# Flamingo block with block-sparse feed-forward: tile 0's maxima added on TensorE instead of by DMA, tile 1's scores ahead of tile 2's queries, weights split one step later

## The reference

```python
q = layernorm(x); k = v = ctx                      # 16 heads of 16 features
s = q @ k.T / 4, masked causally                   # per head, 128 x 128
x = x + tanh(g_xattn) * softmax(s) @ v
n = layernorm(x)
mask = top_4_of_16(softmax(n @ w_router + b_router))      # blocks of 64 hidden units
x = x + tanh(g_ffn) * (relu(n @ w1.T + b1) * mask) @ w2.T + b2-term
```

## Time and profile before

| | before |
|---|---|
| median of 3 runs | 681.2 us (681.01, 681.2, 684.17) |
| profiled execution, own time | 680.97 us |
| span of its instructions | 679.1 us |
| granted TensorE clock, mean | 0.997 |
| TensorE matmul busy | 659.7 us, 97% |
| VectorE busy | 527.8 us, 78% |
| ScalarE busy | 538.9 us, 79% |
| GpSimd busy | 556.0 us, 82% |

### The profile page before, as it was taken

The page is one execution under the profiler, slowest core; times in us unless marked ns, Lnnn a source line. Parts: engine busy times, 40 slices in busy tenths (PEclk is TensorE's granted clock), DMA queues, the critical chain, the costliest instruction groups (busy, mean ns, idle before and its releaser), DMA issues.

```text
span 679.1 us, 30579 instructions
## 1 busy us (share of the span) xinstructions
PE 659.7 (97%) x12960; PEld 611.9 (90%) x12960; DVE 527.8 (78%) x1429; ACT 538.9 (79%) x785; POOL 556.0 (82%) x718
## 2 busy tenths in 40 slices
PE   6779999999999999999999999999999999999997
PEld 5668899999999999999999999989999999999997
DVE  6899887788777778788778878777878877877742
ACT  4668788888888888888888888888888888887732
POOL 6677888988988898888898898888888889887643
PEclk9899999999999999999999999999999999999999
DMA  5323355556545446645556654544554554553110
GB/s 197 96 55 86 88 109 99 116 109 115 120 114 116 99 110 116 111 112 113 100 117 107 116 111 122 103 107 114 113 113 112 116 100 96 98 86 64 28 40 32
DMA packets 192279, 69.24 MB, mean 102 GB/s; under 512 B 166160, under 2 KB 191888, under 8 KB 192144
## 3 DMA queue, kind: packets, MB, share of 16 engines
q1 hardware_dynamic: 191312, 65.72, 45.7%
q10 hardware_dynamic: 832, 1.57, 0.6%
HBM read 19.03 MB, written 8.39 MB: 40 GB/s over the span
## 4 chain that ended last, share of the span: by engine, by line
PE 86%; DVE 5%; DMA 3%; ACT 2%; issue 2%; POOL 1%; SPq 1%; POOLq 0%; DVEq 0%
PE bank L423 11%; PE score_banks L344 10%; PE bank L357 8%; PE score_banks L314 8%; PE bank L425 8%; PE bank L424 8%; PE bank L446 8%; PE bank L447 8%; PE bank L448 8%; PE bank L371 4%; PE bank L401 2%; PE score_banks L327 1%; DMA used_all<-used 1%; PE bank L393 1%; ACT weights L525 1%
## 5 line engine op out<-in xcount | busy, mean ns | idle before, releaser
L880 POOL TENSOR_TENSOR h_low<-hid,h_high 128x512 fp32r<-128x512 f32 x128 | 164.2, 1283 | 12.8 <-ACT hid L560 12.8
L738 DVE SCALAR_TENSOR_TENSOR hid<-bank,b_cols,used_all 128x256 f32<-128x256 f32 x248 | 108.1, 477 | 65.9 <-PE bank L425 58.2
L873 POOL TENSOR_SCALAR_AFFINE_SELECT weights<-weights 128x1024 f32<-128x1024 f32 x128 | 138.2, 1103 | 18.2 <-ACT weights L525 16.4
L423 PE MATMUL bank<-xT_high,w_high 128*128 128x256 f32 x496 | 151.5, 305 | 0.8 <-DVE hid L738 0.7
L525 ACT ACTIVATE weights<-score_banks 128x1024 f32<-128x1024 f32 x128 | 124.3, 1024 | 34.7 <-PE score_banks L344 34.6
L424 PE MATMUL bank<-xT_low,w_high 128*128 128x256 f32 x496 | 139.4, 281 | 0.0
L425 PE MATMUL bank<-xT_high,w_low 128*128 128x256 f32 x496 | 139.4, 281 | 0.0
L446 PE MATMUL bank<-w_high,h_high 128*128 128x256 f32 x488 | 137.3, 281 | 0.7 <-POOL h_low L880 0.7
L447 PE MATMUL bank<-w_low,h_high 128*128 128x256 f32 x488 | 137.7, 282 | 0.0
L448 PE MATMUL bank<-w_high,h_low 128*128 128x256 f32 x488 | 136.2, 279 | 0.0
L423 PEld LDWEIGHTS bank<-xT_high,w_high 128*128 128x128 f32 x496 | 93.3, 188 | 8.9 <-DVE hid L738 1.1
(11 more groups left out here) (105 smaller groups left out, 1411.1 us busy)
## 6 DMA issues: line engine op xcount, KB each, us to landing
x_in<-in_x SPq DMA_DIRECT2D x31, 256.0 KB, 3.1
out_y<-y_out SPq DMA_DIRECT2D x31, 256.0 KB, 2.2
c_in<-in_ctx SPq DMA_DIRECT2D x30, 256.0 KB, 2.8
qT<-qT SPq DMA_DIRECT2D x128, 4.0 KB
w_stage<-in_w1T ACTq DMA_DIRECT2D x1, 1024.0 KB, 9.2
hid<-in_w2T SPq DMA_DIRECT2D x8, 128.0 KB, 2.7
kT_parts<-k_parts SPq DMA_TRANSPOSE x57, 2.8
qT_parts<-q_parts SPq DMA_TRANSPOSE x57, 2.7
```

The lines of the kernel that those rows point to most:

```text
L423: pe.matmul(out=bank, lhsT=w1_high[:, k, c], rhs=high, start=k == 0, stop=False)
L738: dve.scalar_tensor_tensor(hid[:, n % 4, j], hid_bank(n)[:, j * TOKS:(j + 1) * TOKS], b1_cols[:, c:c + 1], used_all[:, p % 2], ALU.add, AL ...
L873: pool.affine_select(out=w, in_=w, compare_op=ALU.is_ge, fill=0.0, base=0, pattern=[[0, 2 * HB], [1, S]], channel_multiplier=-1).then_inc( ...
L880: pool.tensor_tensor(h_low[:, p % 2, chunks], hid[:, n % 4], h_high[:, p % 2, chunks].bitcast(F32), ALU.subtract).then_inc(h_low_made, 1)
```

## The change

For tile 0 alone the maxima no longer ride in tile 2's queries, and no DMA brings them. `row_maximum(0)` writes them into a tile of their own, `first_ride`, zero elsewhere. TensorE copies `qT` of tile 0 into a bank with one product by the identity (`first_again`) and accumulates onto it eight products of `first_ride` by halves of the identity (`first_maximum`). ScalarE copies the sum back over `qT` of tile 0 (`first_evacuated`). `shifted_scores(0)` waits for that copy, and so does the first `out_transposed`, which uses the same bank. In iteration 0 TensorE runs `scores(1)` ahead of the transposes of tile 2's queries. `max_row(0)` is gone from SyncE's queue. The pieces of the weights are taken in iterations 1 to 4, two each, and not in iterations 0 to 4.

```diff
+        first_ride = sb("first_ride", [P, HB, U, PAD], F32)
...
         def pieces_of(i):
-            return {0: (0, 1), 1: (2, 3), 2: (4, 5), 3: (6,), 4: (7,)}.get(i, ())
+            return {1: (0, 1), 2: (2, 3), 3: (4, 5), 4: (6, 7)}.get(i, ())
...
             def q_transposed(b):
                 pe.wait_ge(qn_made, b + 1)
-                if b >= MAX_LAG:
+                if b > MAX_LAG:
                     pe.wait_ge(max_found, b - MAX_LAG + 1)
...
+            def first_again():
+                pe.wait_ge(q_copied, 1)
+                pe.matmul(out=banks[M1][:], lhsT=ident[:], rhs=qT[:, 0, :], start=True, stop=False)
+
+            def first_maximum():
+                pe.wait_ge(max_found, 1)
+                for r in range(HB):
+                    f, t = divmod(r, 2)
+                    for g in range(2):
+                        turned = pe.matmul(out=banks[M1][:, r * S + g * HALF:r * S + (g + 1) * HALF],
+                                           lhsT=first_ride[:, 2 * t + g].rearrange("p u d -> p (u d)"),
+                                           rhs=ident[:, f * HALF:(f + 1) * HALF], start=False,
+                                           stop=r == HB - 1 and g == 1)
+                turned.then_inc(first_turned, 1)
...
             def shifted_scores(b):
                 s = b % TS
-                pe.wait_ge(max_landed[s], 2 * 16 * (b // TS + 1))
+                if b == 0:
+                    pe.wait_ge(first_copied, 1)
+                else:
+                    pe.wait_ge(max_landed[s], 2 * 16 * (b // TS + (1 if s else 0)))
...
                         q_transposed(i + 2)
+                    if i + 1 == 0:
+                        first_again()
                 else:
-                    if q_early(i + 2):
+                    if i > 0 and q_early(i + 2):
                         q_transposed(i + 2)
                     if i > 0 and k_early(i + 2):
                         k_transposed(i + 2)
                     if i + 1 < N:
                         scores(i + 1)
                     if i == 0:
+                        first_maximum()
+                        q_transposed(i + 2)
                         k_transposed(i + 2)
...
+            def first_evacuated():
+                act.wait_ge(first_turned, 1)
+                act.copy(qT[:, 0, :], banks[M1][:]).then_inc(first_copied, 1)
...
                 elif i >= 0:
+                    if i == 0:
+                        first_evacuated()
                     if q_early(i + 2):
...
-                ride = q_pad[:, carrier % QS, :, RIDE_COL].rearrange("p (t g u) -> p u t g", g=2, u=U)
+                if b == 0:
+                    dve.wait_ge(first_zeroed, 1)
+                    ride = first_ride[:, :, :, MAX_COL].rearrange("p (t g) u -> p u t g", g=2)
+                else:
+                    ride = q_pad[:, carrier % QS, :, RIDE_COL].rearrange("p (t g u) -> p u t g", g=2, u=U)
...
+            dve.memset(first_ride[:], 0.0).then_inc(first_zeroed, 1)
...
-                if 0 <= i < N:
+                if 1 <= i < N:
                     max_row(i)
```

More of the change, by code:

```diff
@@ L170, in build @@
         tri_made = sem("tri_made")
+        first_zeroed, first_turned, first_copied = (sem(n) for n in ("first_zeroed", "first_turned", "first_copied"))
         numbers_set, filler_set = sem("numbers_set"), sem("filler_set")
```

## The result

The changed kernel takes 684.01 us (median of 14 runs, 682.35 to 686.79) beside 681.91 us of the kernel before (14 runs, 680.09 to 684.17): ratio 1.0033, interval 1.0017 to 1.0048, which is 1.2 to 3.3 us. It is slower by 2.1 us, not by 0.3, and beyond the top of the range (682.7).

What follows compares the result with a forecast made beforehand. The engine-hopping chain bounds the front, VectorE's queue to `route` gates iteration 4, TensorE bounds from 75 us. 680.97 - 1.30 + 0.53 + 0.40 + 0.75 = 681.35 us, stated as median 681.5; range 680.2 to 682.7 us.

Steps and rivals of the forecast that it cites:

- s: Front, up to the end of tile 2's scores: everything runs 1.30 us earlier, summed as 0.72 + 0.54 + 0.04.
- The clock, 0.54 us: Tile 2's scores on TensorE: the clock stays up, so they take 1.18 us instead of 1.72.
- `shifted_scores(0)` at 15.35, 0.72 us: Tile 0's scores against its maxima: they start at 15.35 us instead of 16.07, no longer waiting for the DMA.
- B: Rival: front worth less, clock falls anyway or tile 4's x lands later; 681.9 to 682.8 us, chance 0.22.
- The later terms: Iterations 3 and 4: wait for GpSimd's piece 0.53, slower `xn` 0.40, second subtraction 0.75; 1.68 us given back.
- the pair's bounds: VectorE's two subtractions before `route`, iteration 4: 1.37 to 1.96 us, so 0.35 to 0.94 more; 0.75 taken.
- D: Rival: no change at the front, because tile 4's x holds tile 1's maxima, which `shifted_scores(0)` awaits; chance 0.01.
- A: Rival: the front's gain survives, as GpSimd does not delay `xn` and the pair costs least; 679.7 to 680.9 us, chance 0.25.
- the coincidence of 0.1 us: Iteration 4: `xn` meeting GpSimd's next instruction and so running slowly depends on timing this close.
- C: Rival: six loads queued earlier delay w1's landing; over 0.5% slower only if 7 us late; chance 0.02.

Runs made afterwards that it cites:

- second profile after: The changed kernel, unchanged, profiled once more: 683.69 us.
- third profile after: The changed kernel, unchanged, profiled a third time: 684.46 us.

## Why the prediction was wrong, step by step

**The step that failed is s, the gain at the front, 1.30 us.** It came to nothing (medians 41.13 and 41.20 us for tile 5's scores). Both of its terms failed, and a cost that it left out came on top.

*The clock, 0.54 us.* The clock in the two windows did what was forecast (1.00 and 1.00), and the tile's scores took 1.18 us. But they were not on the path to the next step: TensorE stopped, by the reading above for its next 16 KB of instructions, and went on 3.3 to 3.6 us behind their start at either clock. The first profile before has this stop too, 0.54 us at 22.72 with "issue" as its releaser, and the prediction does not mention it. It was the slack into which the gain went. The 18 records that the change puts ahead of the stop were priced only where they run; they also move the stop up, so that more of the product stands behind it. In the second profile after, the stop of 1.66 us was followed by the 1.2 GHz level from 24 to 28 us, and the scores against the maxima at 23.58 were followed by the next ones 7.5 us later instead of 6.9. That fall is the cost that the sum did not have.

*`shifted_scores(0)` at 15.35, 0.72 us.* `first_maximum` is as priced, 2.00 us with its tail for 16 records (1.83 us to the next row, a pitch of 0.114). But the start lay at 15.59 to 16.09 us in six of the seven profiles with these products in which the clock was up; the seventh, 16.98, stands behind a stop in added transposes. In the second profile after VectorE's maxima of tile 1 release it (0.15 us of waiting at 16.01), and they hang on the load of x, which landed at 13.17 us there instead of 12.56. B named that, with more loads in the queue as the reason; but the landing varies in both kernels, 12.37 to 12.81 us in the three profiles before and 12.02 to 13.17 in the three after. And the 16.07 from which the term is counted is not the rule. Only in the first profile is the DMA last. In five others of the kernel before and its versions the same maxima of tile 1 come last, and with the clock up at 10 us one of them starts at 15.69. The products replace a transfer that only one of these profiled executions waited for. Where the clock is down around 10 us, as in two profiles of three of the changed kernel, `first_again` takes 1.6 to 1.9 us instead of the 0.9 to 1.2 allowed, is hidden by nothing, and the start is 17.06 to 17.38 us. The kernel before suffers there too (16.69, 17.94). The falls there come behind waits of 1.22 to 1.75 us ahead of the first scores, but waits up to 1.51 us also passed without one. These waits vary from run to run in both kernels (0.75 to 1.75); the prediction took one profile as the rule.

**The later terms were near, and one was missing.** Against the start of tile 5's scores, before and after: `xn(2)` starts 3.33 and 3.87 us behind it, +0.54 (forecast 0.53); from `xn` to the subtraction 0.32 and 0.73, +0.41 (0.40); the subtractions 1.02 and 1.82, +0.80 (0.75); from there to `route` 0.85 and 1.23, +0.38 (not forecast). The missing one is `xT_low`, 0.76 us beside GpSimd's mask, which started ahead of it at 50.41. It was 0.39 us before, when the mask began at 46.14, behind it. The sum is +2.13 us with 1.68 forecast; the ruler says +2.12.

The choice within the pair's bounds was good. The Trainium skill's rule (SBUF — State Buffer, Who interferes with whom), that a VectorE instruction with two SBUF inputs and a GpSimd instruction that reads SBUF exclude each other, is borne out here: `k_parts` took 1.07 us between the two subtractions instead of 0.68, the upper course. The missing term fits the same rule.

**The rivals.** B's outcome came, by its own condition ("as soon as s is below 1.68"), but beyond its price (681.9 to 682.8 us with s = 0.72) and mostly by other means: the clock stayed up where B had it fall, 17 to 21 us, and no rival had TensorE's own stop. D, with a chance of 0.01, had the better mechanism for the term of 0.72 us: the maxima of tile 1 hold `shifted_scores(0)` in both kernels. It was dismissed because 15.25 is 0.8 us ahead of 16.07, which is true of the first profile alone. With s = 0 and 2.12 us of later terms it comes to 680.97 + 2.12 = 683.09 on the profiled scale, 684.0 against the median that was measured beside it. A, the gain survives, had nothing for it: there was little gain, and the coincidence of 0.1 us did occur. C did not occur. In the profiles the reverse is seen: with the products and the old table w1's casts stand ahead of the exponentials and tile 2's scores waited 2.01 and 3.31 us (1.1 us in the three profiles after), and with the new table no cast waits for w1. That advantage of the change was not priced. The range was also too narrow because the median of three runs before, 681.2, was 0.7 below the one of 14.

**What stays open.** Why the packet of instructions came about 3 us earlier in the third profile after, and how much of the spread in time is due to it, to w1's landing and to the clock; they come together and were not separated. That the front's gain is exactly zero is read from three profiles of each kernel, whose starts of tile 5's scores lie 2.6 and 3.3 us apart; a few tenths either way are possible. Only the 2.12 us are the same in every profile. The four versions of the changed kernel with the ruler back at 7.2 to 7.4 us still took 683.3 to 684.0 us, each with a wait or a queue elsewhere in its profile; only the move of piece 4 shows its gain in the time as well. So the queue is the measured place of the loss, and what these other versions lose instead is argued from one profile each.

## What to carry to other kernels

When work is moved to a later step, price the queue of that step term by term, with every instruction of GpSimd that runs beside it; here that sum was forecast as 1.68 us, measured as 2.12 and decided the result. A gain at the front must be followed to the next wait of the same engine, "issue" included: a stop in the middle of a run of equal instructions, with no semaphore, stood here at one place in the code behind a packet of instructions, and gains ahead of it ended there. Profile a short, latency-bound front more than once before a tenth of a microsecond of it enters a sum.

## What was not expected of the hardware

- TensorE stops in the middle of equal products, by all signs for its instructions: 0.5 to 1.9 us in tile 0's product with the values in 12 of the 18 profiles, 2.3 to 2.9 us behind a packet of 16 KB. A second such place stands in the router's product, 0.88 us at 47.73 in the changed kernel, where the kernel before shows none. The versions with transposes added to hold the clock up have such stops of 0.5 to 1.4 us at other places.
- The first 40 us of one and the same program are not one fixed course: tile 5's scores started at 40.26 to 42.85 us before and 40.84 to 44.14 us after, and the times of these profiled executions lay 3.4 and 3.1 us apart.
- GpSimd and VectorE hold each other up in both directions: `k_parts` 0.68 to 1.07 us, `xT_low` 0.39 to 0.76 us, `xn` 0.41 to 0.81 us.
